# Routing before the core products in one mixture of experts; returned rows and half of the next norm inside another

## The reference

```python
# layer 1, feed-forward ("first expert stage"): 8 experts, top 2, all of them computed densely
h = x @ down_w + down_b                       # 256 -> 128, "narrow"
logits = x @ router_w + router_b - COST_LAMBDA * cost
probs = softmax(logits); topv, topi = top_k(probs, 2); gate = softmax(topv)
for k in range(2):                            # mask = one_hot(topi[..., k])
    acc = sum_e gelu(gelu(h * mask_e) @ w1_e + b1_e) @ w2_e + b2_e
    out += acc * gate[..., k:k+1]
out += 0.1 * (gelu(gelu(h) @ shared_w1 + shared_b1) @ shared_w2 + shared_b2)
out = out @ up_w + up_b
out = out + (gelu(x) @ core_w + core_b)       # "core products"

# layer 2, feed-forward ("second expert stage"): 16 experts, top 4, and a shared one
routed = einsum('enh,ne->nh', y, comb)        # y = silu(g) * u @ w_down, each expert on its tokens
shared = silu(h @ sh_gate) * (h @ sh_up) @ sh_down
x = x + routed + sigmoid(h @ sh_gate_w) * shared
# layer 3, attention: grouped query attention on layernorm(x)
```

## Time and profile before

| | |
|---|---|
| median of 3 runs | 1224.74 us (1219.68 to 1227.09) |
| profiled execution, its own time | 1227.9 us |
| its span in the profile | 1225.8 us |
| PE busy | 1075.1 us, 88% of the span |
| DVE busy | 776.5 us, 63% |
| ACT busy | 572.5 us, 47% |
| POOL busy | 385.0 us, 31% |
| mean granted TensorE clock | 0.96 |

### The profile page before, as it was taken

The page is one execution under the profiler, slowest core; times in us unless marked ns, Lnnn a source line. Parts: engine busy times, 40 slices in busy tenths (PEclk is TensorE's granted clock), DMA queues, the critical chain, the costliest instruction groups (busy, mean ns, idle before and its releaser), DMA issues. The chain is left out here.

```text
span 1225.8 us, 22586 instructions
## 1 busy us (share of the span) xinstructions
PE 1075.1 (88%) x8177; PEld 663.4 (54%) x8192; DVE 776.5 (63%) x2357; ACT 572.5 (47%) x1193; POOL 385.0 (31%) x499
## 2 busy tenths in 40 slices
PE   5789899968999889899998898988888979976898
PEld 2447644647755534456665454556666545553465
DVE  6833487575678344667885787642334576969855
ACT  3859345753526434264554465325323134538443
POOL 2535303000003200044665256156665113862000
PEclk9889999989989899999998999999999999986999
DMA  9100000000050030000000000545555400000001
GB/s 369 46 1 3 1 2 1 1 1 1 1 224 2 1 138 1 1 1 2 3 2 2 1 2 14 224 147 152 151 158 151 138 0 2 3 1 0 1 1 35
DMA packets 23485, 60.73 MB, mean 50 GB/s; under 512 B 3681, under 2 KB 12009, under 8 KB 22480
## 3 DMA queue, kind: packets, MB, share of 16 engines
q1 hardware_dynamic: 18864, 48.92, 11.4%
q0 software_dynamic: 4512, 10.37, 2.9%
HBM read 52.95 MB, written 8.29 MB: 50 GB/s over the span
## 5 line engine op out<-in xcount | busy, mean ns | idle before, releaser
L972 ACT ACTIVATE PT<-PS 128x384 f32<-128x384 f32 (+1 forms) x320 | 153.2, 530 | 160.3 <-PE PS L720 115.9
L871 DVE CUSTOM_DVE_ANT_0 junk<-PS,TRI 128x128 bf16<-128x128 f32 (+1 forms) x384 | 110.9, 352 | 2.4 <-PE PS L701 2.4
L270 PE MATMUL PS<-identb 128*128 128x512 bf16 x370 | 94.0, 391 | 5.5 <-PEq L2184 1.8
L701 PE MATMUL PS<-KS,QM 32*128 32x128 f32 (+1 forms) x768 | 90.1, 344 | 8.8 <-ACT PT L972 1.6
L701 PEld LDWEIGHTS PS<-KS,QM 32*128 32x128 f32 x768 | 73.6, 184 | 41.2 <-issue 21.9
L720 PE MATMUL PS<-QM,KS 32*128 32x256 f32 (+1 forms) x768 | 88.5, 347 | 0.5 <-ACT PT L972 0.2
L1052 POOL TENSOR_TENSOR OD<-OD 128x256 f32<-128x256 f32 x16 | 11.6, 728 | 235.8 <-DVE OD L931 235.8
L1030 POOL TENSOR_SCALAR_AFFINE_SELECT PT<-PT 128x512 f32<-128x512 f32 x96 | 60.6, 638 | 69.6 <-ACT PT L972 69.6
L790 PE MATMUL PS<-PT,VM 128*32 128x256 f32 (+1 forms) x1024 | 72.3, 357 | 9.0 <-POOL PT L1030 8.4
L2289 PE MATMUL PS<-WU,XT 128*128 x188 | 65.9, 474 | 11.2 <-issue 7.6
L1294 POOL TENSOR_TENSOR ROT<-RC,RS 128x512 f32<-128x512 f32 x16 | 20.3, 1271 | 175.1 <-DVE RS L1283 173.7
(11 more groups left out here) (394 smaller groups left out, 2653.8 us busy)
## 6 DMA issues: line engine op xcount, KB each, us to landing
WD<-w2d_in SPq DMA_DIRECT2D x47, 256.0 KB
WU<-w2u_in SPq DMA_DIRECT2D x1, 5632.0 KB, 18.8
WA<-wl_in SPq DMA_DIRECT2D x1, 5137.0 KB, 15.7
GB<-gate_rows SPq DMA_DIRECT2D x8, 512.0 KB, 9.2
WU<-chosen SPq DMA_DIRECT2D x16, 256.0 KB, 6.0
WB<-wb_in SPq DMA_DIRECT2D x1, 3208.0 KB, 18.4
WA<-wa_in SPq DMA_DIRECT2D x1, 2560.0 KB, 16.1
WA<-w2s_in SPq DMA_DIRECT2D x6, 384.0 KB, 16.3
```

The lines of the kernel that those rows point to most:

```text
L270: pe.matmul(PS[:, bank, :].rearrange("p (a n) -> p a n", a=4), identb[:], identb[:].rearrange("p (a n) -> p a n", a=1).to_broadcast([P, 4, ...
L701: return pe.matmul(PS[:, s, m * T:m * T + n], queries(U, v)[rows, m * P:(m + 1) * P], keys(U, v)[rows, 0:n], start=True, stop=True, skip_g ...
L871: last = dve.tensor_tensor_reduce(junk[:, s, m * P:m * T + P], PS[:, s, m * T:m * T + (m + 1) * P], TRI[:, (1 - m) * P:T], 1.0, NEG, ALU.a ...
L972: act.activation(PT[:, g % 3, st_slot(k), 0:W], PS[:, st_bank(g, k), 0:W], ACT.Exp, scale=scale).then_inc(S["at_exp"], 1)
```

## The change

In the first stage PE does the narrow product of chunk 0, the transposes of groups 2 and 3 without fillers, the router's products in two halves, and only then the narrow product of chunk 1. The gates' transposes stand ahead of the core products, with eight fillers ahead of them instead of six. ACT does the first gelu between `root` and the two `copy`, then both exponentials, and only then the second gelu and that of the core. DVE adds up the biases after it has copied the turned gates. POOL's addition of the bias rows waits for the gates as well.

In the second stage each `returned(g)` stands one `mult` earlier. Groups 0 and 1 of layer 3's norm are measured, applied, transposed and copied at the end of the second stage's block, with `pre` first; `project_paired` takes the norm as `begun` and does groups 2 and 3 alone, and its 15 fillers ahead of the projections go (16 stand at the end of the second stage). The banks of the transposes are 0, 1, 6 and 7 instead of 4 to 7.

```diff
@@ project_paired
-            norm = norm_steps(st, X, H, to_HT, tbank=lambda g: 4 + g, **norm_of)
+            norm = norm_steps(st, X, H, to_HT, tbank=lambda g: 4 + g, **norm_of) if begun is None else begun
@@ PE
-                    warm(pe, 3, 8)
-                    norm["turn"](pe, 0)
-                    warm(pe, 3, 4)
-                    norm["turn"](pe, 1)
-                    warm(pe, 3, 3)
+                    if begun is None:
...
@@ DVE; ACT alike with root and copy
+                        for g in range(BEGUN, TT // 2):
+                            norm["measure"](dve, g)
+                        for g in range(BEGUN, TT // 2):
+                            norm["apply"](dve, g)
@@ experts1, PE
-                    for c in range(NCH):
-                        if c:
-                            norm["turn"](pe, 2 * c)
-                            warm(pe, 0, 4)
-                            norm["turn"](pe, 2 * c + 1)
-                            warm(pe, 0, 3)
-                        norm["columns"](pe, 2 * c + 1)
...
-                    for t in range(TT):
...
+                    norm["columns"](pe, 1)
+                    narrow(0)
+                    norm["turn"](pe, 2)
+                    norm["turn"](pe, 3)
+                    route(0)
+                    norm["columns"](pe, 3)
+                    route(1).then_inc(S["route_logits"], 1)
+                    narrow(1)
                     go_up(0)
                     go_up(1)
-                    pe.wait_ge(S["core_gelu"], 1)
-                    for g in range(TT // 2):
-                        core(g)
-
-                    warm(pe, 4, 6)
+                    warm(pe, 5, 8)
                     pe.wait_ge(S["gates"], d["gates"] + 1)
                     for t in range(TT):
                         last = pe.transpose(PS[0:E, 4 + t // 4, ...], G[:, t, :], ident)
                     last.then_inc(S["turned"], 1)
+                    pe.wait_ge(S["core_gelu"], 1)
+                    for g in range(TT // 2):
+                        core(g)
@@ experts1, ACT
+                    norm["root"](act, 3)
+                    narrow_gelu(0)
+                    norm["copy"](act, 2)
+                    norm["copy"](act, 3)
                     act.wait_ge(S["dve_mark"], d["dve_mark"] + 1)
                     act.activation(PRB[:], PRB[:], ACT.Exp).then_inc(S["act_mark"], 1)
-                    for c in range(NCH):
...
-                    act.activation(GX, HT[:], ACT.Gelu).then_inc(S["core_gelu"], 1)
                     act.wait_ge(S["dve_mark"], d["dve_mark"] + 2)
                     act.activation(LG[:], LG[:], ACT.Exp).then_inc(S["act_mark"], 1)
+                    narrow_gelu(1)
+                    act.activation(GX, HT[:], ACT.Gelu).then_inc(S["core_gelu"], 1)
@@ experts1, POOL
                     pool.wait_ge(S["row_sum"], 1)
+                    pool.wait_ge(S["gates"], d["gates"] + 1)
@@ experts2, PE, after the last go_down
+                    warm(pe, 2, 8)
+                    for g in range(BEGUN):
+                        following["turn"](pe, g)
+                        warm(pe, 2, 4)
@@ experts2, DVE
                     mult(FRONT, 1)
+                    returned(0)
                     mult(FRONT + 1, 0)
-                    returned(0)
+                    returned(1)
                     mult(FRONT + 1, 1)
-                    returned(1)
+                    returned(2)
                     mult(FRONT + 2, 0)
-                    returned(2)
+                    returned(3)
                     mult(FRONT + 2, 1)
-                    returned(3)
+                    for g in range(BEGUN):
+                        if g == 0:
+                            dve.wait_ge(S["down_ps"], d["down_ps"] + units(NSH - 1, 0))
+                        following["measure"](dve, g)
+                    for g in range(BEGUN):
+                        following["apply"](dve, g)
@@ layers
-        experts2(following, *scale_work)
+        second = norm_steps(None, X, H, to_HT, tbank=lambda g: (0, 1, 6, 7)[g], begun=False, pre=add_sums(SGC))
+        experts2(following, second, *scale_work)
-                                  "v": wL("v3", KD), "o": wL("o3", KD)}, 16, 0.25, turned=True, pre=add_sums(SGC))
+                                  "v": wL("v3", KD), "o": wL("o3", KD)}, 16, 0.25, turned=True, begun=second)
```

More of the change, by code:

```diff
@@ L1217, in project, with project_paired @@
             done[name] += k
-    def project_paired(w, hd, V, spread, arrived=None, **norm_of):
+    def project_paired(w, hd, V, spread, arrived=None, begun=None, **norm_of):
         cos = cst(f"cos{hd}", 1)
@@ L1237, in _ @@
                         pe.wait_ge(*arrived)
-                    warm(pe, 3, 8)
-                    norm["turn"](pe, 0)
-                    warm(pe, 3, 4)
-                    norm["turn"](pe, 1)
-                    warm(pe, 3, 3)
+                    if begun is None:
+                        warm(pe, 3, 8)
+                        norm["turn"](pe, 0)
+                        warm(pe, 3, 4)
+                        norm["turn"](pe, 1)
+                        warm(pe, 3, 3)
                     for n, (a, _, j, c) in enumerate(work):
@@ L1297, in _ @@
                 def _(act):
-                    norm["scalar"](act)
+                    if begun is None:
+                        norm["scalar"](act)
+                    else:
+                        for g in range(BEGUN, TT // 2):
+                            norm["root"](act, g)
+                        for g in range(BEGUN, TT // 2):
+                            norm["copy"](act, g)
                     for n, (_, query, j, c) in enumerate(work):
@@ L1996, in _, with route @@
                         last.then_inc(S["narrow"], 1)
-                    for t in range(TT):
-                        for k in range(KD):
-                            last = pe.matmul(logits[:, t, :], HT[:, k, t * P:(t + 1) * P], router[:, k, :],
-                                             start=k == 0, stop=k == KD - 1)
-                    last.then_inc(S["route_logits"], 1)
+                    def route(c):
+                        for t in range(TPC * c, TPC * c + TPC):
+                            for k in range(KD):
+                                last = pe.matmul(logits[:, t, :], HT[:, k, t * P:(t + 1) * P], router[:, k, :],
+                                                 start=k == 0, stop=k == KD - 1)
+                        return last
+                    norm["columns"](pe, 1)
[6 more added lines that the diff above has]
+                    narrow(1)
                     go_up(0)
                     go_up(1)
-                    pe.wait_ge(S["core_gelu"], 1)
-                    for g in range(TT // 2):
-                        core(g)
-                    warm(pe, 4, 6)
+                    warm(pe, 5, 8)
                     pe.wait_ge(S["gates"], d["gates"] + 1)
@@ L2027, in _, with narrow_gelu @@
                 def _(act):
-                    norm["scalar_rest"](act)
-                    act.wait_ge(S["dve_mark"], d["dve_mark"] + 1)
-                    act.activation(PRB[:], PRB[:], ACT.Exp).then_inc(S["act_mark"], 1)
-                    for c in range(NCH):
+                    def narrow_gelu(c):
                         act.wait_ge(S["narrow"], c + 1)
@@ L2122, in experts1, with experts2 @@
                 done[name] += k
-    def experts2(norm, sums, over_partitions, scales, replace):
+    def experts2(norm, following, sums, over_partitions, scales, replace):
         tag = str(nc.next_id())
@@ L2183, in experts2 @@
             AHEAD = 3
+            n = NCH * NSH + NBLK
+            for name, k in (("route_logits", 1), ("gates_copied", 1), ("act_mark", 2), ("dve_mark", 1), ("turned", NBLK), ("ht", NBLK),
+                            ("up_ps", n), ("down_ps", n), ("act_out", n), ("mult_out", n), ("x_added", TT + TT * TOP2)):
+                done[name] += k
+            following["begin"]()
             with nc.Block() as block:
@@ L2420, in _ @@
                             silu(i, c)
+                    for g in range(BEGUN):
+                        following["root"](act, g)
+                    for g in range(BEGUN):
+                        following["copy"](act, g)
                 @block.vector
```

21 lines of the change are left out of this document (12 added, 9 removed).

## The result

| | median | runs |
|---|---|---|
| before | 1225.56 us | 4 (1219.68 to 1227.09) |
| changed | 1210.72 us | 4 (1205.69 to 1214.74) |

The ratio is 0.988, with a 95% interval of 0.9855 to 0.9906: 14.84 us less at the median, where 14.6 were forecast. The four runs of the changed kernel spread over 9 us. The profiled execution of the changed kernel took 1214.74 us and has a span of 1212.7 (1225.8 before).

The account below looks back on a forecast made before the run. Engines' waits in the two expert stages, passed on whole by barriers, were taken as the bound. 10.3 us from the first plus 4.3 from the second make 14.6 off 1224.7: 1210.1 us, range 1205 to 1218.

Parts of the forecast that it names:

- 3 idle ahead of the second `go_up`: First stage, PE up to the gates: idle 2.3 us for the second gelu, then eight fillers; gates' transposes end at 418.1.
- step 4: First stage, gate rows' round trip: 7.45 us, back at 425.6, covered by 6.9 us of core products but for 0.6.
- step 5: First stage, loop: the product at 442.99 comes at 432.7; the wait for POOL's addition has a cover of 4 us.
- First term: First expert stage: shorter by 10.3 us, from 442.99 to 432.7.
- Step 6: Second stage: returned rows usable at 964.5, DVE done at 981.6 instead of 983.97, PE's last product ends at 983.5.
- rival B: Second stage: the returned rows land late, at 966.8, losing 2.3 us, total 1212.4 us; chance 0.11.
- Step 7: Layer 3's norm split at the barrier: DVE idle 2.2 us, projection 1 starts at 994.5 instead of 998.84.
- Second term: Second stage and layer 3's entry: 4.3 us gained, 2.0 if the returned rows land only at 966.8.
- A: First stage: the clock falls in PE's new 2.3 us gap, losing 2 us, total 1212.2 us; chance 0.20.
- E: Slower than before: the clock stays low at both stages, 16.4 us lost, total 1226.5 us; chance 0.03.
- C: First stage: each change of function holds ACT 2.66 us instead of 1.30, total 1214.1 us; chance 0.04.
- D: One of the two halves earns nothing: 1214.4 us with only the first stage's gain, 1220.4 with only the second's; chance 0.12.

Follow-up runs that it names:

- Experiment 3: Changed kernel with the core products again ahead of the fillers and the gates' transposes: 1216.91 us, first stage 105.28 us.
- experiment 5: Changed kernel without POOL's added wait for the gates before its addition of the bias rows: 1213.19 us, first stage 98.75 us.
- second kernel: Changed kernel with the old first expert stage, so only the second stage and layer 3's entry are new: 1218.19 us, ratio 0.9957 to the kernel before.
- experiment 1: Kernel before with the new first expert stage alone: 1215.67 us, ratio 0.9922 to the kernel before.
- experiment 4: Changed kernel with each group of returned rows again behind the next multiplication, the norm still inside the second stage: 1212.23 us, tail 41.08 us.
- experiment 7: Changed kernel with group 2 of layer 3's norm also measured inside the second stage: 1211.74 us, entry of layer 3 26.22 us.
- experiment 8: Changed kernel with group 2 of layer 3's norm measured inside the second stage and five instead of eight fillers ahead of the gates' transposes: 1210.15 us.
- experiment 6: Changed kernel with PE's first `go_up` also waiting for the second gelu, for a longer gap: 1215.94 us, first stage 101.09 us.

## Why the prediction was right

The predicted 1210.1 us stand against 1210.72 measured, and faster by over 1% was the likeliest of the three. But the agreement of the totals is better than that of the parts, and to within 0.6 us it is luck, with runs that spread over 9. So here are the steps, for the first stage in us from its start (402.62 in the forecast's count, 406.12 in the changed kernel):

| step | forecast | measured |
|---|---|---|
| 1 logits | 7.0 | 6.87 (412.99) |
| 2 gates ready | 14.1 | 13.92 (420.04) |
| 3 idle ahead of the second `go_up` | 2.3 | 2.25 |
| 3 gates transposed | 15.5 | 15.52 (421.64) |
| 4 end of the core products | 22.4 | 22.2 (428.35) |
| 5 the `go_down` that stood at 442.99 | 30.1 | 29.96 (436.08) |

**First term**: 10.3 forecast, 10.40 measured. Experiment 3 splits it: the covered round trip 6.5, the rest of the new order 3.9. Some 4.3 of the 10.4 us are the clock, which fell at PE's waits of 3.38 us (415.97) and 2.89 us (437.75) before and stays at 1.00 over the whole stretch now. The forecast had them in its sum, since it priced the core products at full clock and let the loop keep its full beat behind them, but in its account of the term it named only the gates and the transfer. In step 4 the wait of 0.6 us for the gate rows didn't show; the products of the shared expert covered it. In step 5 POOL's addition took the same 4.52 us as before; experiment 5 confirms that the added wait is free.

**Step 6**: the returned rows were used 5.83 us after `mult(3, 0)` had started (956.81 - 950.98), 6.43 in the second kernel (958.68 - 952.25); the forecast had 6.4 (964.5 - 958.14), rival B 8.6. In all seven profiles with the new order it was 5.83 to 6.82. DVE was through with the last `mult` after 22.6 us (973.58 - 950.98), forecast 23.5. PE's wait ahead of its last product was 0.96 us, less than the 1.5 to 2 named: the small miss has the same cause. DVE's wait for the rows ended 1.71 us behind the `mult` ahead of it, outside the 2 to 5 named as a sign, since the rows came sooner.

**Step 7**: DVE idle at the barrier 2.33, forecast 2.2. **Second term**: 4.3 forecast; 5.4 between the two profiles, 2.7 to 3.7 against the old tail where the lower clock missed the projection (experiment 1). The forecast lies between the two. It took the tail of one execution as the price of the old code, and 1.7 us of that tail was the clock's fall at a bad moment. What the working did not say is what experiment 4 shows in one execution: moving the norm earns this only together with the earlier returned rows. The two edits were priced in one chain and so came out right. One sign was named wrongly: projection 1 was to come about 4 us nearer to the last returned row's start. It came 1.6 us nearer (16.90, from 969.36 to 986.26, against 18.49, from 980.35 to 998.84), since that row moves forward too; the working's own times give some 17.

**The rivals.** A didn't occur in the profiled execution; the clock was 1.00 through the gap and after, and so it was in experiments 1, 3, 4, 7 and 8. In experiment 6 a fallen clock cost 1.5 us; the forecast had named 2. But the reason that it gave against A fails. It compared the lengths of idle pieces, 3.38 us with a fall behind it and 2.42 without. The windows of the kernel before show the fall inside the piece:

```profile
412.00:414.00 2.00, 0.59 (x6) 0.49 (x5) 0.95 (x5) 0.32 (x2) 0.00 (x0) 1.00 0.00 0
414.00:416.00 2.00, 0.03 (x1) 0.04 (x1) 1.83 (x7) 1.99 (x3) 0.00 (x0) 0.52 0.00 0
```

PE's last product had ended at 412.58, so the clock fell about 1.5 us into the idle piece, and its full length can't have been what brought it down. The changed kernel is idle for 2.25 us, longer than that, and kept 1.00. That A didn't come true is thus not explained by anything in the forecast. Nor did the clock come back within 4 us, as the forecast says under E: it was at 0.54 from 420 to 421, 5 us after PE had resumed.

B fell with the landing times. C fell: the load at 407.45 took 1.28 and its gelu started 0.02 later, at 408.75, and the load at 415.84 was followed at 417.14. The Trainium skill's figure of about 2.66 us for a switch (ScalarE: Activation LUTs, "What ACT_TABLE_LOAD costs") isn't what a switch costs ACT in any of these rows. D fell with experiments 1 and 2. E wasn't seen: the clock was at 1.00 behind the gap of the first stage, and the second stage's end and the entry took what full-speed products take (1.96 us for projection 0 at 981.25, where before it was 3.49).

**What the sum left out.** The start of the program, up to 78.28 us before and 81.80 in the changed kernel, took 3.5 us longer, though no edit touches it, and so the profiled spans differ by only 13.1. The granted clock tells the two apart there. The window over the first products, before, and then the changed kernel:

```profile
34.00:38.00 4.00, 4.00 (x13) 2.14 (x12) 3.23 (x11) 3.88 (x19) 1.78 (x2) 0.85 0.01 2
```

```profile
34.00:38.00 4.00, 4.00 (x8) 1.68 (x7) 3.10 (x11) 4.00 (x20) 1.97 (x2) 0.50 0.07 28
```

With 0.85 and 0.50 of the clock PE did 13 and 8 records in the same 4 us. In the ten profiles the first stage begins anywhere from 399.04 to 406.12, in code that is the same in all. That is as much as the runs of one kernel spread, and why single times (experiments 3 to 7) are read by stretches and not by their totals. The range of 1205 to 1218 allowed for it.

## What to carry to other kernels

A round trip through DRAM that ends in a wait is best covered by work that waits for nothing, so start what feeds the trip as early as it can be had and put the independent products behind its start, not ahead of it. Moving part of a successor's work across a barrier paid here only together with an edit by which the engine that does it is through earlier: ask which instruction stands last on that engine, and move that one first. A wait that is removed can give back more than its length, where the clock had fallen at it: look at the products behind it too. Where the clock comes and goes, price a stretch from more than one execution, and compare stretches that begin at the same piece of work.

## What was not expected of the hardware

- The granted clock fell without an idle piece of PE ahead of it (experiment 5: 0.57 from 412 to 416, with PE idle for no more than 0.2 us at a time ahead of it), and in the kernel before some 1.5 us after PE's last product (1.00 from 412 to 414, 0.52 from 414 to 416). It stayed at 1.00 over an idle piece of 2.25 us in the changed kernel. What decides it wasn't settled.
- A DVE instruction on one element per partition, `cc` (L2117), with two operands in SBUF, took 1.80 us beside POOL's addition and ended 0.02 us after it (424.76 and 424.74); alone it took 0.16. In the eighth kernel it started at 416.21 and took 2.26 us, with the end at 418.47; POOL's addition ended at 418.45 (413.93 and 4.52). In experiments 1, 4 and 7 it took 1.80, 1.80 and 1.81 us and ended 0.02 us after POOL too. So a DVE instruction of 0.16 us was held up to the end of POOL's, while the copy of the gates out of PSUM ran beside the same addition in its usual 1.21 us. The Trainium skill (SBUF — State Buffer, "Who interferes with whom") says that a DVE instruction with two SBUF inputs contends with a GpSimd instruction that reads SBUF, since its second input comes through the read interface that they share, and calls contention on the shared ports an exclusive lock; the traces agree, in that DVE waits out POOL's whole instruction, while POOL's 4.52 us stay as they were. It cost nothing here, since 3.5 us lay between DVE's first product for the shared expert (425.7) and the `go_down` that uses it (429.21).
